# TensorE walks the turns over the edges in loops, and six turns move from the mixing stage to the key stage

## The chip, the cores and the metric

The kernel runs on one core of a Trainium2 chip. Its metric is the time of one execution on the device in microseconds; three runs of the kernel before gave 1978.74, 1978.78 and 1986.1 us, so its median is 1978.78 us. The engines are called by the profile's names: PE (TensorE, with its weight loads as PEld), DVE (VectorE), ACT (ScalarE), POOL (GpSimd) and SP (the engine that only issues transfers here). Each has its own queue of instructions, and they wait for each other by counting semaphores.

## The reference, cut to what matters

N = 6250 nodes have 256 values each; E = 100000 edges carry a source and a destination, sorted by destination. The destinations are drawn as 6250 u^2, so the low nodes have many edges and the high ones few.

```python
xn = layernorm(x)                                    # (6250, 256)
neigh_sum = segment_sum(xn[src], dst)                # sum of the sources' rows for each destination
neigh_mean = neigh_sum / maximum(degree, 1)
g = relu(concat([xn, neigh_mean]) @ W + b); g = g / norm(g)

q, k, v = split(rmsnorm(xn) * g_pre @ w_qkv)         # 4 heads of 32
q = softmax(q, over the 32 of a head) * scale
k = softmax(k, over all nodes and 4 memory columns)
context = k^T v                                      # one 32 x 32 per head
mix = rmsnorm((q @ context) @ w_out + b_out) * g_out + xn

x = x + g + mix
x = x + top_2_of_8_experts(layernorm(x))             # 256 -> 1024 -> 256, gelu
```

The softmax of k runs over all nodes. So the context needs the keys of all 49 tiles of 128 nodes, and the outputs can begin only after it.

## The kernel before, in words

**The gather.** The kernel first normalises x and multiplies it by the lower half of W; the result z lies in HBM. POOL then gathers the rows of z in order of the edges: 784 indirect transfers of 128 rows (L695), four of which make a quad. 196 quads go one after the other into a ring of 8 slots in SBUF. POOL waits before a quad until the turn that last used its slot is counted in p_ready, and it counts the quads that have landed in quads_in.

**A turn.** A turn adds one quad's rows to one tile of 128 destinations. DVE compares the edges' destinations with 0 to 127 and so builds a 0/1 matrix (L1292, four turns ahead), PE multiplies it with the quad's rows (L1813, four fp32 matmuls, which the trace shows as eight), and DVE adds the result to the tile's row in SBUF (L1307). A quad that spans two tiles is used in two turns, so there are 196 + 48 = 244 turns, numbered 0 to 243. Where a turn's quad lies in the ring, and how many quads must have landed, is only known on the chip; PE reads both from a table into registers, eight turns at a time (the loads are recorded at L1800). The PE sequence of a turn is the function turn (it begins with the test j % REGS at L1799), with waits for quads_in, s_built (the matrix) and acc_done (the add of four turns ago).

**What the turns are woven into.** PE, DVE, ACT and SP have their order written out by hand, and the turns stand between the work of two stages.
- The key stage goes over the 49 tiles. Per tile ACT normalises x (L766), PE transposes it (turn_a, L1823), ACT copies it out (L886), SP stores it for later (L501), PE multiplies it to keys and values (kv, L1830), ACT copies these (L890) and DVE keeps the running maximum (L1341). The tiles 1 to 48 carry turns 0 to 89: two each, but every eighth tile only one (turns_of_a, A_EVERY = 8).
- The context has 7 groups of tiles, with the turns 90 to 95 between them.
- The mixing stage goes over the 49 tiles again. Per tile SP loads the normalised tile (L520), PE makes queries and the node's own product (qu, L1879), DVE and ACT make the softmax, PE turns the queries (L1884) and multiplies the ones of the tile before by the context (mix_out, L1889), and DVE and ACT finish the output. Each tile carries three turns: 96 to 242. Tiles 11 to 26 also fold a bias (bfold, L1894). Turn 243 stands at the end.

In the key stage and the context each turn is followed by a small matmul on a spare bank (follow, L1794). After the turns come routing and 56 expert tiles, for which all engines already have a loop over pairs of tiles (the function repeat; its turn back is recorded at L100).

In the kernel before PE's part of the key and mixing stages is written out tile by tile. The other engines' parts of it are, too, and they stay so.

## Time and profile before

| | us |
|---|---|
| median of the runs | 1978.78 |
| span of the profiled execution | 2187.37 |
| of it before the first turn | 89 |
| key stage with turns 0 to 89 | 507 |
| context with turns 90 to 95 | 58 |
| mixing stage with turns 96 to 243 | 636 |
| routing | 206 |
| expert tiles | 691 |

The profiled execution has no other time than its span; it is 208.6 us longer than the median of the runs. The stretches are cut by hand at round times of the trace. Busy time in the profile doesn't count instructions that only wait, branch, compute in registers or issue a transfer; these appear under an engine's queue (PEq, PEldq, SPq). The idle time before an instruction is put down to the one that released it; "issue" is idle time in which nothing is seen to be waited for, and "remote" one whose releaser the profile doesn't find.

### The profile page before, as it was taken

What the parts mean: (1) busy time and instruction counts of PE and PEld (TensorE: products, weight loads), DVE (VectorE), ACT (ScalarE), POOL (GpSimd) and SP (SyncE); (2) the same over time, 40 slices, a digit from 0 to 9 for tenths busy, and PEclk for the clock granted to TensorE, in tenths of its full rate; (3) what the DMA queues carried; (4) which work ended last, traced back from release to release, by engine and by line L of the source; (5) the groups of instructions that cost most, each with busy time, mean ns of one, the idle gap of its engine ahead of it and who ended that gap; (6) DMA issues with size and microseconds to landing.
All of it is one profiled execution on the core that took longest, in us unless ns stands there. A gap on an engine that the chain in (4) does not pass through costs nothing.

```text
span 2187.4 us, 33907 instructions
## 1 busy us (share of the span) xinstructions
PE 1583.7 (72%) x9422; PEld 1361.2 (62%) x9423; DVE 1101.1 (50%) x3043; ACT 900.9 (41%) x1840; POOL 1140.4 (52%) x1141
## 2 busy tenths in 40 slices
PE   6735536546566667867767763548999999999998
PEld 5524435435454544545545543447999999999997
DVE  6512212212234536655555457765666666666664
ACT  6501101101112323323334336554666666666664
POOL 3267666666656666666666612555333333333333
PEclk9868868767878979988888785558999999999999
DMA  7334333333324655566656526537878777877775
GB/s 210 119 100 114 104 101 107 101 97 103 106 81 154 224 165 182 182 180 184 198 182 189 181 76 197 188 135 248 228 215 220 213 221 208 226 214 221 213 221 137
DMA packets 188123, 368.85 MB, mean 169 GB/s; under 512 B 33324, under 2 KB 134172, under 8 KB 173656
## 3 DMA queue, kind: packets, MB, share of 16 engines
q0 software_dynamic: 77296, 252.50, 41.3%
q1 hardware_dynamic: 102992, 113.64, 16.3%
q10 hardware_dynamic: 7736, 1.52, 0.4%
q8 instruction: 45, 0.74, 0.1%
q14 instruction: 54, 0.44, 0.1%
HBM read 287.94 MB, written 80.39 MB: 168 GB/s over the span
## 4 chain that ended last, share of the span: by engine, by line
PE 50%; another core or an unknown queue 17%; DVE 12%; issue 11%; DMA 5%; ACT 3%; SPq 2%; POOL 0%; DVEq 0%; ACTq 0%; POOLq 0%
PE bank L1813 11%; PE bank L2002 5%; PE bank L2003 5%; PE bank L2004 5%; PE bank L2025 5%; PE bank L2024 5%; PE bank L2026 5%; PE bank L1879 3%; DMA xTs<-xnT_d 3%; PE bank L1830 2%; PE bank L1973 1%; DVE acc_lent L1478 1%; DMA z_d<-w2s_lent 1%; DVE acc_lent L1307 1%
## 5 line engine op out<-in xcount | busy, mean ns | idle before, releaser
L695 POOL DMA_INDIRECT w2s_lent<-z_d,edge_tabs_lent x784 | 777.5, 992 | 438.7 <-issue 256.7
L1307 DVE TENSOR_TENSOR acc_lent<-acc_lent,bank 128x258 f32 x244 | 102.7, 421 | 600.6 <-remote 348.8
L1813 PE MATMUL bank<-w2s_lent,S_lent 128*128 x976 | 261.0, 416 | 19.0 <-issue 9.5
L1031 ACT ACTIVATE G<-bank,acc_lent 128x256 f32<-128x256 f32 x448 | 188.3, 472 | 205.9 <-DVE w2s L1670 124.5
L1813 PE MATMUL bank<-w2s_lent,G 128*128 x976 | 265.9, 422 | 3.4 <-issue 3.4
L2024 PE MATMUL bank<-w2s 128*128 128x256 f32 x896 | 264.4, 295 | 0.0
L2002 PE MATMUL bank<-w2s,acc 128*128 128x256 f32 x896 | 260.4, 291 | 2.8 <-issue 2.8
L739 POOL DMA_INDIRECT out_dram<-G,acc_lent x112 | 179.6, 1604 | 158.3 <-DVE G L1650 117.3
L1629 DVE TENSOR_TENSOR acc<-w1s,acc 128x512 fp32r<-128x512 f32 x224 | 155.1, 693 | 200.7 <-ACT acc L1000 174.1
L2004 PE MATMUL bank<-w2s,acc 128*128 128x256 f32 x896 | 254.0, 284 | 0.0
L2025 PE MATMUL bank<-w2s 128*128 128x256 f32 x896 | 253.7, 283 | 0.4 <-issue 0.4
L2026 PE MATMUL bank<-w2s 128*128 128x256 f32 x896 | 253.2, 283 | 0.9 <-issue 0.9
L2003 PE MATMUL bank<-w2s,acc 128*128 128x256 f32 x896 | 253.5, 283 | 0.0
L1813 PEld LDWEIGHTS bank<-w2s_lent,S_lent 128*128 128x128 f32 x976 | 202.5, 211 | 72.6 <-issue 38.5
L1813 PEld LDWEIGHTS bank<-w2s_lent,G 128*128 128x128 f32 x976 | 207.3, 215 | 55.3 <-issue 18.9
L890 ACT ACTIVATE w1s<-bank,r 128x256 f32<-128x256 f32 x49 | 23.3, 475 | 463.8 <-remote 335.0
L723 POOL DMA_DIRECT2D w2s<-w_d x112 | 64.7, 579 | 272.3 <-PE bank L2026 259.5
L1823 PE MATMUL bank<-ident,w2s_lent 128*128 128x128 f32 x98 | 23.7, 330 | 230.0 <-ACT w2s_lent L766 120.2
L2002 PEld LDWEIGHTS bank<-w2s,acc 128*128 128x128 f32 x896 | 171.4, 191 | 3.0 <-issue 2.8
L2026 PEld LDWEIGHTS bank<-w2s 128*128 128x128 f32 x896 | 172.0, 192 | 1.8 <-issue 1.8
L2003 PEld LDWEIGHTS bank<-w2s,acc 128*128 128x128 f32 x896 | 172.9, 193 | 0.0
L2025 PEld LDWEIGHTS bank<-w2s 128*128 128x128 f32 x896 | 171.6, 191 | 1.5
(322 smaller groups left out, 2993.3 us busy)
## 6 DMA issues: line engine op xcount, KB each, us to landing
w2s<-w_d POOLq DMA_DIRECT2D x112, 1024.0 KB
w_d<-w2s_lent SPq DMA_DIRECT2D x64, 256.0 KB
acc_lent<-bucket_d SPq DMA_DIRECT2D x56, 266.0 KB
w2s_lent<-z_d,edge_tabs_lent POOLq DMA_INDIRECT x784
bu_d<-w2s_lent SPq DMA_DIRECT2D x98, 128.0 KB
w2s_lent<-bu_d SPq DMA_DIRECT2D x14, 768.0 KB
w1s<-in_L_ffn_W_dram SPq DMA_DIRECT2D x8, 1024.0 KB
w2s_lent<-in_L_ffn_W_dram SPq DMA_DIRECT2D x32, 256.0 KB
```

Source lines behind the costliest of these rows:

```text
L695: pool.indirect_dma_start(out=ring_rows[:, row % (RING * QUAD), 0:D], out_offset=None, in_=z_d[:, :], in_offset=bass.IndirectOffsetOnAxis( ...
L739: pool.indirect_dma_start(out=out[:, :], out_offset=bass.IndirectOffsetOnAxis(ap=nid[par][:, j:j + 1], axis=0), in_=ys[par][:, j, :], in_o ...
L1031: g = act.activation(raw[q % 2][:, k * MT:(k + 1) * MT], bank[q][:, k * MT:(k + 1) * MT], ACT.Gelu, bias=b1c[1 - par][:, 2 * q + k:2 * q + ...
L1307: dve.tensor_tensor(to, to, bank[j % DEPTH][:, 0:ACCW], ALU.add).then_inc(s["acc_done"], 1)
L1629: dve.tensor_tensor(w1lo[:, :, cols].bitcast(F32R), w1_part(e, q), w1hi[:, :, cols], ALU.subtract).then_inc(s["w1_ready"], 1)
L1813: m = pe.matmul(bank[j % DEPTH][:, 0:ACCW], S_of[j % DEPTH][:, k, :], rows[:, ds(bases[j], ACCW)], start=(k == 0), stop=(k == QUAD - 1))
L2002: pe.matmul(to, hi, x_hi, start=(k == 0), stop=False)
L2003: pe.matmul(to, hi, x_lo, start=False, stop=False)
L2004: m = pe.matmul(to, lo, x_hi, start=False, stop=(k == DC - 1))
L2024: pe.matmul(to[j], hi, w_hi, start=False, stop=False, skip_group_check=True)
L2025: pe.matmul(to[j], hi, w_lo, start=False, stop=False, skip_group_check=True)
L2026: m = pe.matmul(to[j], lo, w_hi, start=False, stop=(c == HC - 1), skip_group_check=True)
```

## The change

TensorE's order for the key stage becomes a function over four tiles that is written out once and then looped 11 times; that of the mixing stage is written out for tiles 1 to 10, looped over 4 times four tiles with the fold and 5 times four tiles without it (the first of each written out), and written out again for the last three. In a loop the numbers that the waits compare with depend on the loop's register, so they are computed in registers. The loads of a turn's place and count move to the head of each group of four or five tiles.

For the loop each tile of the key stage has to have the same number of turns: two. The stage thus takes turns 0 to 95, the context 96 to 101, and the mixing stage begins with turn 102; its first six tiles (SHORT = 6) have two turns and the others three. The numbers follow on all engines, so DVE's order changes as well. The eight matmuls that turn the folded bias stand ahead of tile 27 on PE, and not behind it.

```diff
@@ -408,10 +408,14 @@
 
         def turns_of_a(t):
 
-            return range(2 * t - t // A_EVERY, 2 * (t + 1) - (t + 1) // A_EVERY)
+            return range(2 * t, 2 * t + 2)
+
+        def first_turn_of_b(t):
+
+            return B_FIRST + 3 * t - SHORT if not isinstance(t, int) or t >= SHORT else B_FIRST + 2 * t
 
         def turns_of_b(t):
-            return range(B_FIRST + 3 * t, B_FIRST + 3 * t + 3)
+            return range(first_turn_of_b(t), first_turn_of_b(t + 1))
 
         def in_range(i, ahead):
 
@@ -1437,7 +1441,8 @@
                 b_q2(t)
                 if t:
                     b_o1(t - 1)
-                turn(mine[2])
+                for j in mine[2:]:
+                    turn(j)
                 if SPLIT_AT < t <= SPLIT_END:
                     split_w2(t - SPLIT_AT - 1)
                 if t:
@@ -1792,28 +1797,26 @@
             def follow(spare=7):
 
                 pe.matmul(bank[spare][:, 0:P], before[:, :], ones_b[:, :], start=True, stop=True)
-            bases, needs = {}, {}
-
-            def turn(j):
-
-                if j % REGS == 0:
-                    _, loaded = nc.values_load_multi_w_load_instructions(
-                        rows_i[0:1, base_at + j:base_at + j + REGS], engines=[mybir.EngineType.PE], min_val=0, max_val=(RING - 1) * QW_RING,
-                        skip_runtime_bounds_check_because="a slot of the ring, times the width of one")
-                    bases.update({j + k: v for k, v in enumerate(loaded)})
-                    _, loaded = nc.values_load_multi_w_load_instructions(
-                        rows_i[0:1, need_at + j:need_at + j + REGS], engines=[mybir.EngineType.PE], min_val=1, max_val=QUADS,
-                        skip_runtime_bounds_check_because="a quad's number plus one")
-                    needs.update({j + k: v for k, v in enumerate(loaded)})
-                pe.wait_ge(s["quads_in"], needs[j] & COUNT)
+            regs = {}
+
+            def turn_registers(first, n):
+
+                for what, at, low, high in (("base", base_at, 0, (RING - 1) * QW_RING), ("need", need_at, 1, QUADS)):
+                    _, regs[what] = nc.values_load_multi_w_load_instructions(
+                        rows_i[0:1, ds(at + first, n)], engines=[mybir.EngineType.PE], min_val=low, max_val=high,
+                        skip_runtime_bounds_check_because="a slot of the ring times the width of one, or a quad's number plus one")
+
+            def turn(j, k, bank_of, spare=True):
+
+                pe.wait_ge(s["quads_in"], regs["need"][k] & COUNT)
                 pe.wait_ge(s["s_built"], j + 1)
                 until(pe, s["acc_done"], j + 1 - DEPTH)
-                for k in range(QUAD):
-                    rows = ring[:, k * ACCW:(RING - 1) * QW_RING + (k + 1) * ACCW]
-                    m = pe.matmul(bank[j % DEPTH][:, 0:ACCW], S_of[j % DEPTH][:, k, :], rows[:, ds(bases[j], ACCW)],
-                                  start=(k == 0), stop=(k == QUAD - 1))
+                for q in range(QUAD):
+                    rows = ring[:, q * ACCW:(RING - 1) * QW_RING + (q + 1) * ACCW]
+                    m = pe.matmul(bank[bank_of][:, 0:ACCW], S_of[bank_of][:, q, :], rows[:, ds(regs["base"][k], ACCW)],
+                                  start=(q == 0), stop=(q == QUAD - 1))
                 m.then_inc(s["p_ready"], 1)
-                if j < B_FIRST:
+                if spare:
                     follow()
 
@@ -1832,13 +1835,17 @@
             pe.wait_ge(s["consts_dve"], 3)
             pe.wait_ge(s["kv_weights"], 1)
             turn_a(0)
-            for i in range(NT - 1):
-                mine = turns_of_a(i)
-                turn(mine[0])
-                turn_a(i + 1)
-                for j in mine[1:]:
-                    turn(j)
-                kv(i)
+
+            def four_tiles_a(m):
+
+                turn_registers(8 * m, 8)
+                for k in range(4):
+                    i = 4 * m + k
+                    turn(2 * i, 2 * k, 2 * k % DEPTH)
+                    turn_a(i + 1)
+                    turn(2 * i + 1, 2 * k + 1, (2 * k + 1) % DEPTH)
+                    kv(i)
+            repeat(pe, None, four_tiles_a, 0, (NT - 1) // 4)
             kv(NT - 1)
             pe.wait_ge(s["kv_dve"], NT)
@@ -1858,8 +1865,9 @@
                                   kv_all[0:rows, ds(8 * g + j, 1), HID:KVW].rearrange("p o w -> p (o w)"),
                                   start=False, stop=last, skip_group_check=True)
                 m.then_inc(s["ctx_mm"], 1)
+            turn_registers(CTX_FIRST, 6)
             for g in range(6):
-                turn(CTX_FIRST + g)
+                turn(CTX_FIRST + g, g, (CTX_FIRST + g) % DEPTH)
                 ctx_mm(g)
...
-            for t in range(NT):
-                mine = turns_of_b(t)
-                f = t - FOLD_AT
-                if f == 0:
-                    pe.wait_ge(s["w1_in"], 16 * EXPERTS)
+
+            def tile_b(t, k, j, n=3, bank_of=0, fold=None):
+
                 qu(t)
-                turn(mine[0])
-                if t:
-                    mix_out(t - 1)
-                turn(mine[1])
-                if 0 <= f < 2 * EXPERTS:
-                    bfold(f // 2, f % 2)
-                turn(mine[2])
+                turn(j, k, bank_of, spare=False)
+                mix_out(t - 1) if not isinstance(t, int) or t else None
+                turn(j + 1, k + 1, (bank_of + 1) % DEPTH, spare=False)
+                if fold:
+                    bfold(*fold)
+                if n == 3:
+                    turn(j + 2, k + 2, (bank_of + 2) % DEPTH, spare=False)
                 turn_q(t)
-                if f == 2 * EXPERTS:
-                    pe.wait_ge(s["bf_evac"], 2 * EXPERTS)
-                    for c in range(HC):
-                        m = pe.matmul(bank[5][:, c * EXPERTS:(c + 1) * EXPERTS], bacc[0:EXPERTS, c * P:(c + 1) * P], ident[0:EXPERTS, 0:EXPERTS],
-                                      start=True, stop=True)
-                    m.then_inc(s["b1_mm"], 1)
+
+            def plain_tiles_b(first, end):
+
+                j0, j1 = first_turn_of_b(first), first_turn_of_b(end)
+                turn_registers(j0, j1 - j0)
+                for t in range(first, end):
+                    mine = turns_of_b(t)
+                    tile_b(t, mine[0] - j0, mine[0], len(mine), mine[0] % DEPTH)
+
+            def four_tiles_b(first, m, fold=False):
+
+                j = first_turn_of_b(first) + 12 * m
+                turn_registers(j, 12)
+                for k in range(4):
+                    tile_b(4 * m + (first + k), 3 * k, j + 3 * k, 3, (first_turn_of_b(first) + 3 * k) % DEPTH,
+                           (2 * m + k // 2, k % 2) if fold else None)
+            for first in range(0, FOLD_AT, 5):
+                plain_tiles_b(first, first + 5)
+            pe.wait_ge(s["w1_in"], 16 * EXPERTS)
+            repeat(pe, None, lambda m: four_tiles_b(FOLD_AT, m, True), 0, EXPERTS // 2)
+            pe.wait_ge(s["bf_evac"], 2 * EXPERTS)
+            for c in range(HC):
+                m = pe.matmul(bank[5][:, c * EXPERTS:(c + 1) * EXPERTS], bacc[0:EXPERTS, c * P:(c + 1) * P], ident[0:EXPERTS, 0:EXPERTS],
+                              start=True, stop=True)
+            m.then_inc(s["b1_mm"], 1)
+            repeat(pe, None, lambda m: four_tiles_b(AFTER_FOLD, m), 0, (NT - AFTER_FOLD) // 4)
+            plain_tiles_b(AFTER_FOLD + (NT - AFTER_FOLD) // 4 * 4, NT)
             mix_out(NT - 1)
-            turn(TURNS - 1)
+            turn_registers(TURNS - 1, 1)
+            turn(TURNS - 1, 0, (TURNS - 1) % DEPTH, spare=False)
             pe.wait_ge(s["acc_done"], TURNS)
 
...
-CTX_FIRST = B_FIRST - 6
-A_EVERY = (NT - 1) // (2 * (NT - 1) - CTX_FIRST)
+CTX_FIRST = 2 * (NT - 1)
+B_FIRST = CTX_FIRST + 6
+SHORT = B_FIRST + 3 * NT - (TURNS - 1)
 
 # ---- launch: one core; inputs and outputs as the reference has them ----
```

Three places show what moves. The first is VectorE in the key stage, at the eighth tile. acc_lent is the sum of all tiles, bank3 the result of a turn from PE, the comparison to G builds the matrix of a later turn, and L1341 (L1345 after) is the tile's maximum. Before:

```order
L1341 TENSOR_TENSOR w2s_lent<-w1s,w2s_lent 128x128 [waits kv_dve,kv_act]
L1307 ISA [waits acc_done,p_ready]
L1307 TENSOR_TENSOR acc_lent<-acc_lent,bank2 128x258
L1292 TENSOR_TENSOR G<-iota,edge_tabs_lent 128x512
L1341 TENSOR_TENSOR w2s_lent<-w1s,w2s_lent 128x128 [waits kv_dve,kv_act]
```

After:

```order
L1345 TENSOR_TENSOR w2s_lent<-w1s,w2s_lent 128x128 [waits kv_dve,kv_act]
L1311 ISA [waits acc_done,p_ready]
L1311 TENSOR_TENSOR acc_lent<-acc_lent,bank2 128x258
L1296 TENSOR_TENSOR G<-iota,edge_tabs_lent 128x512
L1311 ISA [waits acc_done,p_ready]
L1311 TENSOR_TENSOR acc_lent<-acc_lent,bank3 128x258
L1296 TENSOR_TENSOR G<-iota,edge_tabs_lent 128x512
L1345 TENSOR_TENSOR w2s_lent<-w1s,w2s_lent 128x128 [waits kv_dve,kv_act]
```

The eighth tile has a second add and comparison ahead of its maximum.

The second place is TensorE at the end of the first mixing tile; bank6 takes the turned queries and bank4 the queries of the next tile. Before, from the last matmul of the second turn (bank1) over the third (bank2):

```order
L1813 MATMUL bank1<-w2s_lent,S_lent 128x258
L1808 REGISTER_ALU
L1813 ISA [waits acc_done,s_built,quads_in]
L1813 MATMUL bank2<-w2s_lent,G 128x258
L1813 ISA
L1813 MATMUL bank2<-w2s_lent,G 128x258
L1813 ISA
L1813 MATMUL bank2<-w2s_lent,G 128x258
L1813 ISA
L1813 MATMUL bank2<-w2s_lent,G 128x258
L1884 MATMUL bank6<-ident,w2s_lent 128x128 [waits q_ready]
L1879 MATMUL bank4<-w2s_lent,xTs 128x384 [waits qu_evac,xb_in]
```

After, from the last matmul of the first turn (bank2) over the second (bank3):

```order
L1816 MATMUL bank2<-w2s_lent,G 128x258
L1811 REGISTER_ALU
L1816 ISA [waits acc_done,s_built,quads_in]
L1816 MATMUL bank3<-w2s_lent,G 128x258
L1816 ISA
L1816 MATMUL bank3<-w2s_lent,G 128x258
L1816 ISA
L1816 MATMUL bank3<-w2s_lent,G 128x258
L1816 ISA
L1816 MATMUL bank3<-w2s_lent,G 128x258
L1892 MATMUL bank6<-ident,w2s_lent 128x128 [waits q_ready]
L1887 MATMUL bank4<-w2s_lent,xTs 128x384 [waits qu_evac,xb_in]
```

There is no third turn, and the transpose of the queries follows the second.

The third place is TensorE at the head of a group of mixing tiles, tile 11. Before:

```order
L1879 MATMUL bank4<-w2s_lent,xTs 128x384 [waits qu_evac,xb_in,w1_in]
L1879 MATMUL bank4<-w2s_lent,xTs 128x384
L1808 REGISTER_ALU
L1813 ISA [waits acc_done,s_built,quads_in]
L1813 MATMUL bank2<-w2s_lent,G 128x258
L1813 ISA
```

After, in the loop:

```order
L1805 TENSOR_LOAD w2s_lent
L1805 ISA
L1805 TENSOR_LOAD w2s_lent
L1884 ISA
L85 REGISTER_ALU [waits xb_in]
L1887 MATMUL bank4<-w2s_lent,xTs 128x384 [waits qu_evac]
L1887 MATMUL bank4<-w2s_lent,xTs 128x384
L1811 REGISTER_ALU
L1812 REGISTER_ALU [waits quads_in]
L85 REGISTER_ALU [waits s_built]
L1816 ISA [waits acc_done]
L1816 MATMUL bank2<-w2s_lent,G 128x258
```

The loads stand ahead of the tile, and the one instruction that waited for three semaphores has become three.

## Rows read from the trace of the kernel before

**Rows 1.** The page: busy time, share, instructions; a DMA queue: packets, MB, share.

```profile
PE 1583.7 (72%) x9422; PEld 1361.2 (62%) x9423; DVE 1101.1 (50%) x3043; ACT 900.9 (41%) x1840; POOL 1140.4 (52%) x1141
...
q8 instruction: 45, 0.74, 0.1%
```

**Rows 2.** Busy time in stretches: from:to, length, then each engine (instructions).

```profile
core 0: us, PE busy (x) PEld busy (x) DVE busy (x) ACT busy (x) POOL busy (x), PEclk, DMA share, GB/s
...
89.00:596.00 507.00, 260.16 (x1100) 207.84 (x1100) 107.93 (x241) 59.18 (x143) 341.29 (x347) 0.76 0.37 104
596.00:654.00 58.00, 33.18 (x172) 25.99 (x172) 18.00 (x34) 9.47 (x12) 35.16 (x34) 0.76 0.29 83
654.00:1290.00 636.00, 453.29 (x1570) 314.96 (x1569) 345.38 (x936) 215.38 (x390) 401.09 (x405) 0.85 0.58 179
...
1496.00:2187.00 691.00, 676.50 (x5607) 671.47 (x5605) 437.05 (x905) 440.12 (x884) 253.85 (x231) 0.99 0.78 215
```

**Rows 3.** Groups by line: busy us, mean ns | idle us before, by releaser.

```profile
L695 POOL DMA_INDIRECT w2s_lent<-z_d,edge_tabs_lent x784 | 777.5, 992 | 438.7 <-issue 256.7 <-remote 88.0 <-PE bank L1813 77.6
```

**Rows 4.** Timeline, 113 to 158 us: start, us, instruction [idle before <-releaser].

```profile
113.66 1.08 PE L1830 MATMUL bank<-G,xTs 128*128 128x256 f32 x4
...
120.59 0.22 PE L1794 MATMUL bank<-ones_b,before 128*128 128x128 bf16 x1
...
149.68 0.95 POOL L695 DMA_INDIRECT w2s_lent<-z_d,edge_tabs_lent  x1 [0.30 <-issue]
...
153.76 0.47 ACT L890 ACTIVATE w1s<-bank,r 128x256 f32<-128x256 f32 x1 [47.84 <-remote]
...
157.47 1.16 POOL L695 DMA_INDIRECT w2s_lent<-z_d,edge_tabs_lent  x1 [6.85 <-remote]
```

**Rows 5.** Waits: who for whom, us in total, times, longest us.

```profile
DVE acc_lent L1307 <- remote: 348.8, 45, 27.0
ACT w1s L890 <- remote: 335.0, 20, 47.8
...
POOL w2s_lent L695 <- issue: 256.7, 667, 33.6
```

**Rows 6.** Timeline around 414 us, PE's key matmuls.

```profile
411.74 1.08 PE L1830 MATMUL bank<-G,xTs 128*128 128x256 f32 x4
...
416.48 1.08 PE L1830 MATMUL bank<-G,xTs 128*128 128x256 f32 x4
```

**Rows 7.** Query matmuls of mixing tiles 1, 2 and 7; idle time before all.

```profile
652.64 2.67 PE L1879 MATMUL bank<-w2s_lent,xTs 128*128 128x384 f32 x4 [0.46 <-DVE w2s_lent L1384]
...
661.92 1.46 PE L1879 MATMUL bank<-w2s_lent,xTs 128*128 128x384 f32 x4
...
735.38 2.13 PE L1879 MATMUL bank<-w2s_lent,xTs 128*128 128x384 f32 x3
...
  DMA xTs<-xnT_d: 78.1, 32
```

**Rows 8.** By source line, PE's queue: duration ns min/median/max, first and last start.

```profile
L100 PEldq FUSED_REGOPS  x24: 68/68/68, 1574.2 to 2132.8; - x24
...
L100 PEldq ALU_OP  x24: 32/32/32, 1598.4 to 2156.7; - x24
L100 PEldq COMPARE_BRANCH  x24: 76/213/238, 1598.5 to 2156.8; - x24
...
L85 PEldq EVENT_SEMAPHORE  x585: 51/51/4847, 14.8 to 2165.5; - x195
...
L1800 PEldq TENSOR_LOAD <-w2s_lent x31: 587/592/1007, 90.8 to 1288.2; - x31
```

**Rows 9.** Timeline of the expert loop where PE turns back.

```profile
1719.83 0.28 PE L2003 MATMUL bank<-w2s,acc 128*128 128x256 f32 x1
1719.95 0.28 PE L2004 MATMUL bank<-w2s,acc 128*128 128x256 f32 x1
```

**Rows 10.** DMA issues: KB each, median us from issue to landing.

```profile
small<-in_L_mix_g_pre_dram ACTq DMA_DIRECT2D x2, 0.5 KB, 2.1
```

More of the change, by code:

```diff
@@ L2079 @@
 AFTER_FOLD = FOLD_AT + 2 * EXPERTS
-B_FIRST = TURNS - 1 - 3 * NT
-CTX_FIRST = B_FIRST - 6
-A_EVERY = (NT - 1) // (2 * (NT - 1) - CTX_FIRST)
+CTX_FIRST = 2 * (NT - 1)
+B_FIRST = CTX_FIRST + 6
+SHORT = B_FIRST + 3 * NT - (TURNS - 1)
 _INS = ["x", "src", "dst", "L0_gnn_W", "L0_gnn_b", "L0_mix_w_qkv", "L0_mix_mem_kv", "L0_mix_w_out", "L0_mix_b_out",
```

## The prediction, made before the result was known

> **What bounds the kernel now.** I read the page's busy shares first: over the span of 2187.4 us no engine is full, TensorE has 72% and POOL 52% [rows 1]. So the kernel has stages with different limits, and the table of stretches comes next [rows 2]. The reader is to see there five parts that the prediction can leave alone or not. The first 89 us (normalisation) and everything after 1290 us (206 us of routing, 691 us of expert tiles with 676.5 us of TensorE busy) hold no turn. All turns lie in the three stretches between: the key stage, 507 us; the context, 58 us; the mixing stage, 636 us.
>
> In these 1201 us the list by line gives POOL's gathers, 784 of them at 992 ns, with 438.7 us idle before them [rows 3]. The timeline shows that 0.30 us of idle time stands before each gather even when nothing holds it [rows 4]. So a gather costs 0.99 + 0.30 = 1.29 us, a quad (four gathers) 5.17 us, and all 784 cost 1013 us. 235 us of the 438.7 are this pace; the wait list has one of 33.6 us, the idle time before the first gather; the other 170 us are waits for a free ring slot [rows 5]. POOL is thus at its own pace for 1013 of some 1183 us from the first gather to the last, and what TensorE does in this time counts only as far as it lets the ring fill.
>
> What fills it is seen in the timeline around 117 to 157 us [rows 4]. TensorE's rows end at 120.8 us, but ScalarE sees the end of the key matmul of 113.66 us only at 153.76 us, after 47.84 us of idle time that the profile can't put down to a queue. TensorE's next transposes wait for ScalarE behind that, the turns wait behind the transposes, eight quads fill the ring, and POOL stands still for 6.85 us. The ring swallowed 41 of these 48 us. Such late ends are the largest entries of the wait list: 348.8 us on the adds of VectorE and 335.0 us on ScalarE's copies of keys [rows 5]. The trace doesn't show their cause, and I assume that the change doesn't touch it.
>
> When it isn't held, TensorE is much quicker than POOL: two key tiles in a row start their key matmuls 4.74 us apart (411.74 and 416.48 us) [rows 6], where the key stage has 507 / 48 = 10.56 us a tile. In the mixing stage the distance is small: 636 / 49 = 12.98 us a tile, against 9.3 us between the first two tiles [rows 7], which is the shortest the first ones show. There the load of the next tile stands in the chain: the query matmuls sat idle 78.1 us for it, 32 times [rows 7].
>
> **The moved turns.** Key tiles 8, 16, ... 48 get a second turn: six turns more, 96 instead of 90. Mixing tiles 1 to 6 lose one each, and from the seventh on every tile starts with the same turn as before. Each turn takes eight matmul records, one add and one comparison that builds the matrix for four turns later; all of these are only moved, and so are the quads that they need. At POOL's pace the total doesn't change, so the term is 0. Its two ends are these. Upper: a turn costs the key stage its own pace of 507 / 90 = 5.63 us, 33.8 us for six, and the mixing stage gives nothing back, since its tiles have another limit: +33.8 us. Lower: the key stage is paced by its tiles (10.56 us whether with one turn or two) and the six turns are free, while the mixing stage gives back 12.98 / 3 = 4.33 us each: -26.0 us. I take 0, since POOL's 1013 us are by far the largest row of this stretch. The first six mixing tiles took 735.4 - 652.6 = 82.8 us, 13.8 us each [rows 7]; with two turns their gathers need at most 2 x 5.17 = 10.3 us a tile, and 9.3 us has been reached with three turns, so TensorE can keep up; a shortfall of some us goes into the ring, which holds 8 x 5.17 = 41 us.
>
> On VectorE the removed turn takes 0.42 + 0.69 us out of the tile, ahead of the work on the output of the tile before, and on the key side the same two instructions stand before the maximum of the tile; both are under the gathers. SP and POOL issue what they did, in the same order.
>
> **The loops.** Nothing of TensorE's arithmetic is added. By the listing of the order, four key tiles had 42 register instructions and loads of registers in a row and now have 68 in a pass; four mixing tiles had 64 and now have 98 (with the fold) or 88. With 11, 3 and 4 passes after the ones that are written out, that is 286 + 102 + 96 = 484 more. In this kernel such instructions take 32 ns (ALU) to 51 ns (wait) each [rows 8], together 15.5 to 24.7 us, and 18 turns back at 32 + 213 + 68 ns add 5.6 us. Against it the pairs of loads fall from 31 to 26, at 592 ns a load: -5.9 us. So this edit lies between -5.9 us (all else hidden) and +30.3 us (all of it on the path). I take +2 us. What hides it: TensorE's queue runs ahead of the matmuls wherever no wait holds it, and where one holds it, the instructions before the wait are done in that time. The expert loop, which is written in the same way, shows it: its matmuls follow each other without idle time at the turn back (1719.83 to 1720.31 us) [rows 9]. Only the two or three instructions behind the last wait of a turn are late, and behind them stands POOL's pace. If that cover is gone, every turn pays about 0.1 us.
>
> The Trainium skill has a rule that speaks against this edit ("Runtime: NRT & Kernel Launch", Instruction fetch mechanics): "A taken branch whose target isn't in the current 2-page window forces a DMA fetch of the target page before execution can continue". By it every pass could begin with a stall. The rows of the existing loop say otherwise for a body of this size: its 24 branches took 76 to 238 ns [rows 8]. With that the sum stays as it is.
>
> One wait moves: the eight small matmuls that turn the folded bias now stand before the queries of tile 27, not behind its turns, and so wait for VectorE's last fold (a few us, once). What is queued behind is that tile; the ring hides it. 0 us.
>
> **Sum.** 2187.4 + 0 + 2 = 2189.4 us on the profiled execution. The runs have a median of 1978.8 us, 208.6 us less than the profile's span, and the profile doesn't tell from which stage they are missing. 1978.8 minus the stretches without turns (986 us) leaves 993 us for what took 1201 us; even without one ring wait the gathers' 1013 us would fill that, which is one more reason for POOL's pace. If the missing time is in the gathers themselves, the mixing stage is nearer to its tile limit, and the moved turns can cost. I carry the +2 us over unscaled: 1981 us.
>
> **The rivals.**
> First, slower: the mixing tiles are bound by their own chain, not by POOL. Place: the first six tiles and the 28 looped ones. The key stage pays 33.8 us for its six turns, the first mixing tiles give back no more than (13.8 - 9.3) x 6 = 27 us, and a looped tile has 34 / 4 = 8.5 instructions more, 0.43 us at 51 ns, 12 us over 28. Together +19 us: 1998 us. It decides once a tile's chain is longer than the 10 to 13 us of its gathers. For it: the 78.1 us before the query matmuls, and the unknown pace of the unprofiled gathers. Against it: 12.98 us a tile against 9.3.
> Second, faster: the key stage is paced by the late ends that come once a tile, not by gathers. Then its second turns are free and the mixing stage gives back 26 us: 1953 us; half of it, 1966 us. For it: 335.0 us of ScalarE's idle time [rows 5]. Against it: POOL is at its pace for 448 of the stage's 507 us (347 gathers at 1.29) [rows 2].
> Third, faster: the late ends come from the long stream of instructions, and loops shorten it. A third of the 170 us of ring waits would be 57 us: 1922 us. Only the size of that wait speaks for it; the page has 45 instruction packets, and none of 0.74 MB in all looks like a load [rows 1].
> Fourth, slower: each of the 18 turns back waits for code to be loaded. The nearest small load of the page took 2.1 us [rows 10], so 38 us less what the ring hides: up to 2017 us. The 238 ns speak against it. This is the mechanism of the Trainium skill's rule quoted above.
>
> **How the numbers follow.** The bound between a change and none is 0.5%, 9.9 us, about what a measurement of this kernel tells. Chances: the forecast 0.46, the first rival 0.27, the second 0.19, the third 0.04, the fourth 0.04. The second and third make the 0.23 for faster, the first and fourth the 0.31 for slower, the forecast the 0.46 for the same. The forecast's own range is 1971 to 1991 us. The range for 8 in 10 must reach into both main rivals: down to 1953, the lower end of the moved turns, and up to 2009, the first rival's 1998 and a part of the loops' upper end: 1953 to 2009 us.
>
> **What would show it.** In the new profile the sum of the stretches of key, context and mixing stage should stay within 10 us of 1201 us, with the boundary between key and mixing stage some 25 to 34 us later and the first six mixing tiles at 9 to 11 us each. Ring waits should stay near 170 us, the branches of the new loops under 0.3 us. The step on the moved turns is wrong if the boundary moves and the last gather moves with it, or if it doesn't move at all. The step on the loops is wrong if idle time before the turns' matmuls put down to nothing ("issue") grows by more than 10 us. The whole is wrong if the late ends become rarer or more frequent, for then 170 us are open in either direction.

## The result, and the profile after

The changed kernel takes 2017.41 us (median of 4 runs, 2010.52 to 2020.09), the kernel before 1978.76 us; the ratio is 1.0179, with a 95% interval of 1.0159 to 1.0198. It is 38.65 us slower. The forecast of 1981 us was wrong, and the time lies outside the range of 1953 to 2009 us.

The profiled execution of the changed kernel has a span of 2015.7 us, as long as its runs. That of the kernel before had been 208.6 us longer than its runs. So the two can't be subtracted stage by stage. The kernel before was profiled a second time (experiment e1), and this second profile (span 1982.7 us) is the one to compare with. Busy time of the changed kernel:

```profile
PE 1600.3 (79%) x9428; PEld 1362.4 (68%) x9429; DVE 1101.1 (55%) x3043; ACT 898.7 (45%) x1840; POOL 1139.1 (57%) x1141
```

TensorE has 1600.3 us, VectorE 1101.1 us and POOL 1139.1 us, almost what they had [rows 1]. Most of the loss is idle time. The stretches of the changed kernel in the order key stage, context, mixing stage, then routing and experts (from:to, length, busy time of each engine, clock, DMA share, GB/s):

```profile
89.00:553.00 464.00, 314.00 (x1164) 232.44 (x1164) 120.07 (x266) 62.12 (x149) 347.91 (x358) 0.84 0.41 118
553.00:585.00 32.00, 26.45 (x156) 22.19 (x157) 13.37 (x21) 6.21 (x7) 24.99 (x24) 0.92 0.32 92
585.00:1172.00 587.00, 440.43 (x1562) 309.89 (x1562) 347.01 (x954) 220.73 (x405) 404.01 (x404) 0.87 0.63 194
1172.00:1320.00 148.00, 74.99 (x550) 69.05 (x551) 119.68 (x621) 99.64 (x244) 83.17 (x85) 0.54 0.61 201
1320.00:2015.00 695.00, 679.77 (x5659) 675.25 (x5657) 440.66 (x921) 444.86 (x893) 260.48 (x240) 0.99 0.77 218
```

The same stretches of the kernel before, in its second profile, which answer to [rows 2]:

```profile
89.00:528.00 439.00, 300.11 (x1119) 222.98 (x1120) 114.66 (x255) 62.92 (x149) 327.79 (x339) 0.83 0.42 119
528.00:556.00 28.00, 23.31 (x151) 19.62 (x149) 13.43 (x22) 5.59 (x6) 22.21 (x20) 0.99 0.31 90
556.00:1135.00 579.00, 449.19 (x1607) 313.01 (x1607) 351.03 (x958) 221.49 (x405) 427.39 (x427) 0.90 0.66 203
1135.00:1290.00 155.00, 82.39 (x592) 76.06 (x593) 122.88 (x638) 102.56 (x249) 87.44 (x89) 0.53 0.60 196
1290.00:1982.00 692.00, 676.96 (x5617) 672.48 (x5616) 439.44 (x912) 442.19 (x889) 255.75 (x236) 0.99 0.79 218
```

The key stage with its six more turns is 25 us longer, the context 4 us, and the mixing stage, which has six turns fewer, is 8 us longer and not shorter. After it the changed kernel needs 843 us and the kernel before 847. So 37 us are lost ahead of routing and none behind it (the two spans differ by 33 us, the medians by 38.65).

Who waits for whom in the mixing stage tells what bounds it (us in total, times, longest). The kernel before, second profile:

```profile
POOL w2s_lent L695 <- issue: 117.7, 346, 5.2
PE bank L1813 <- POOLq L683: 56.4, 23, 6.2
PE bank L1879 <- DMA xTs<-xnT_d: 53.5, 21, 6.9
```

The changed kernel:

```profile
POOL w2s_lent L699 <- issue: 112.6, 332, 5.0
PE bank L1887 <- issue: 64.8, 11, 7.0
PE bank L1887 <- DMA xTs<-xnT_d: 42.6, 16, 4.9
...
POOL w2s_lent L699 <- PE bank L1816: 17.9, 13, 4.5
```

Before, TensorE waits 56.4 us for quads (POOLq L683 counts the landed ones): POOL is the slower one, and TensorE has this much to spare with its turns in the old places. After, that wait is gone, and instead 64.8 us stand before 11 query matmuls (L1887), put down to "issue", that is, to nothing seen. Now POOL waits for TensorE (17.9 us in this stage). Over the whole kernel its gathers have this idle time:

```profile
L699 POOL DMA_INDIRECT w2s_lent<-z_d,edge_tabs_lent x784 | 776.9, 991 | 303.8 <-issue 243.8 <-DMA w2s_lent<-z_d,edge_tabs_lent 36.6 <-PE bank L1816 23.4
```

The end of the stage says the same. The last gather of the kernel before starts at 1124.54 us, and the last turn (TensorE, L1813) waits for its quad:

```profile
1124.54 0.95 POOL L695 DMA_INDIRECT w2s_lent<-z_d,edge_tabs_lent  x1 [0.30 <-issue]
...
1129.40 3.63 PE L1813 MATMUL bank<-w2s_lent,G 128*128 x8 [2.35 <-POOLq L683]
```

In the changed kernel the last turn comes 27 us after the last gather, and ten turns are still to be worked off:

```profile
1136.32 0.95 POOL L699 DMA_INDIRECT w2s_lent<-z_d,edge_tabs_lent  x1 [0.30 <-issue]
...
1163.59 3.18 PE L1816 MATMUL bank<-w2s_lent,G 128*128 x8
```

What holds TensorE is found under its queue. The register loads at the head of each group (L1805: durations in ns min/median/max, first and last start), in six stretches of the changed kernel:

```profile
L1805 PEldq TENSOR_LOAD <-w2s_lent x24: 587/591/625, 91.3 to 506.8; - x24
...
L1805 PEldq TENSOR_LOAD <-w2s_lent x2: 830/833/836, 551.8 to 552.7; - x2
...
L1805 PEldq TENSOR_LOAD <-w2s_lent x2: 2415/2420/2426, 586.1 to 588.6; - x2
...
L1805 PEldq TENSOR_LOAD <-w2s_lent x2: 1342/1444/1547, 639.2 to 640.8; - x2
...
L1805 PEldq TENSOR_LOAD <-w2s_lent x18: 2864/3063/4273, 696.9 to 1085.0; - x18
...
L1805 PEldq TENSOR_LOAD <-w2s_lent x2: 2169/2170/2172, 1129.9 to 1132.1; - x2
```

The loads of eight in the key stage take 0.59 us, as before [rows 8]. The six at the context take 0.83, the 10 from entry 102 2.4, the 14 from 112 1.4, the 12 of each group of four tiles 3.1, the 9 from 234 2.2 us. The number doesn't explain it (14 are quicker than 9), the start does: 8m, 96 and 112 are multiples of four, 102, 234 and the loops' 126, 138, ... aren't. At the head of a group this is seen on TensorE at 745 us:

```profile
744.98 0.32 PE L1892 MATMUL bank<-ident,w2s_lent 128*128 128x128 f32 x1
751.99 2.92 PE L1887 MATMUL bank<-w2s_lent,xTs 128*128 128x384 f32 x4 [6.69 <-issue]
...
763.33 1.46 PE L1887 MATMUL bank<-w2s_lent,xTs 128*128 128x384 f32 x4
```

The turned queries (L1892) are done at 745.3 us, and the next tile's queries begin 6.7 us later, behind a pair of loads of 2.9 and 3.5 us. The gap costs a little more than itself. The four query matmuls behind it take 2.92 us, those of the tile after it, without a gap, 1.46 us. TensorE's granted clock stood at its full level (1.00, 2.4 GHz) before the gap and at the lower one (0.50, 1.2 GHz) behind it:

```profile
740.00:745.00 5.00, 5.00 (x20) 2.62 (x18) 3.89 (x13) 0.31 (x1) 3.77 (x5) 1.00 0.89 267
752.00:755.00 3.00, 3.00 (x5) 1.79 (x6) 0.00 (x0) 0.00 (x0) 2.08 (x4) 0.50 0.93 271
```

### The profile page after: what moved, and what is told of

Same layout as the page of the kernel before. It is cut to its first block, busy times and chain, and to the rows that moved or that the text cites. A ratio compares the mean times of both kernels' runs of the same rounds, so it can differ in the third digit from the quotient of the medians.

```text
span 2015.7 us, 34258 instructions
## 1 busy us (share of the span) xinstructions
PE 1600.3 (79%) x9428; PEld 1362.4 (68%) x9429; DVE 1101.1 (55%) x3043; ACT 898.7 (45%) x1840; POOL 1139.1 (57%) x1141
## 4 chain that ended last, share of the span: by engine, by line
PE 44%; DVE 7%; DMA 7%; issue 5%; SPq 2%; ACT 2%; POOL 1%; DVEq 0%; POOLq 0%; ACTq 0%
PE bank L1816 5%; PE bank L2030 5%; PE bank L2031 5%; PE bank L2032 5%; PE bank L2053 5%; PE bank L2052 5%; PE bank L2054 5%; DMA xTs<-xnT_d 5%; PE bank L1887 3%; PE bank L2001 1%; POOL bucket_d L713 1%; SPq L545 1%; PE bank L1902 1%; PE bank L2041 1%; DVE w2s_lent L1420 1%
## 5 line engine op out<-in xcount | busy, mean ns | idle before, releaser
L1816 PE MATMUL bank<-w2s_lent,G 128*128 x976 | 284.3, 443 | 79.8 <-POOLq L687 76.6
L1816 PE MATMUL bank<-w2s_lent,S_lent 128*128 x976 | 267.0, 422 | 65.2 <-POOLq L687 59.0
L1816 PEld LDWEIGHTS bank<-w2s_lent,G 128*128 128x128 f32 x976 | 213.9, 224 | 147.2 <-issue 109.5
L1816 PEld LDWEIGHTS bank<-w2s_lent,S_lent 128*128 128x128 f32 x976 | 201.5, 211 | 125.1 <-issue 90.6
L1887 PE MATMUL bank<-w2s_lent,xTs 128*128 128x384 f32 x196 | 101.8, 655 | 107.4 <-issue 64.8
L2030 PEld LDWEIGHTS bank<-w2s,acc 128*128 128x128 f32 x896 | 170.3, 190 | 5.4 <-issue 5.4
L2053 PEld LDWEIGHTS bank<-w2s 128*128 128x128 f32 x896 | 171.6, 191 | 1.5
L2052 PEld LDWEIGHTS bank<-w2s 128*128 128x128 f32 x896 | 172.1, 192 | 0.0
L2054 PEld LDWEIGHTS bank<-w2s 128*128 128x128 f32 x896 | 172.0, 192 | 0.0
```

The lines of the kernel that those rows point to most:

```text
L1816: m = pe.matmul(bank[bank_of][:, 0:ACCW], S_of[bank_of][:, q, :], rows[:, ds(regs["base"][k], ACCW)], start=(q == 0), stop=(q == QUAD - 1))
L1887: m = pe.matmul(bank[4][:, 0:HID + D], xTs[:, c * P:(c + 1) * P], w_qu[:, c, :], start=(c == 0), stop=(c == DC - 1))
L2030: pe.matmul(to, hi, x_hi, start=(k == 0), stop=False)
L2052: pe.matmul(to[j], hi, w_hi, start=False, stop=False, skip_group_check=True)
L2053: pe.matmul(to[j], hi, w_lo, start=False, stop=False, skip_group_check=True)
L2054: m = pe.matmul(to[j], lo, w_hi, start=False, stop=(c == HC - 1), skip_group_check=True)
```

## The experiments

Two theories stood against each other after the result. A: the register loads of the mixing stage are slow because of where they start, and take TensorE's spare time. B: the six moved turns cost in the key stage and aren't given back. A third, C, was the loops' register instructions and turns back. All ratios are to runs of the kernel before on the same chip, taken together with those of the experiment; the interval is of 95%. The diffs are cut to the lines that matter, and `...` stands for what is left out.

**e1, the kernel before once more.** No edit.

> The kernel before, unchanged, for a second profile. The first profile was 208.6 us longer than its runs, the changed kernel's only as long as its runs. If the late matmul ends (348.8 us before VectorE's adds put down to nothing) belong to that one profiled execution, this profile has a span near 1977 us, a gather stretch of about 1010 us (784 x 1.29) and no such waits. If they belong to the long stream of written-out instructions, they come again and the span is again near 2187 us. Time: 1979 us in both.

Measured: 0.9993 (0.9979 to 1.0008), span 1982.7 us, gathers from 90.6 to 1125.5 us:

```profile
L695 POOL DMA_INDIRECT w2s_lent<-z_d,edge_tabs_lent x784 | 777.4, 992 | 291.1 <-issue 244.8 <-DMA w2s_lent<-z_d,edge_tabs_lent 41.1 <-PE bank L1813 5.2
```

POOL has 291.1 us idle against 438.7 [rows 3]; of it 33.6 us stand ahead of the first gather, and the waits put down to TensorE are 5.2 us, none longer than the 0.3 us that stand before every gather. The late ends of [rows 4, 5] don't come again, though the instruction stream is the same. They belonged to that one execution.

**e2, mixing loads from multiples of four.** In the changed kernel:

```diff
             def turn_registers(first, n, skip=0):
+                n = (n + skip + 3) // 4 * 4
...
-                        rows_i[0:1, ds(at + first, n)], ...
+                        rows_i[0:1, ds(at + first - skip, n)], ...
+                    regs[what] = regs[what][skip:]
...
-                turn_registers(j, 12)
+                turn_registers(j, 12, first_turn_of_b(first) % 4)
```

> The changed kernel, but each register load of the mixing stage begins at a multiple of four entries of the table and takes whole fours (16 entries where it took 12). Theory of the slow loads: the pairs of loads at the 13 heads, 6.0 us each in the changed kernel's profile (2.9 + 3.1), fall to about 1.1 us an instruction, 2.2 us a pair, so some 45 us of PE's time at the tile heads go, and the kernel comes back to 1978 to 1990 us. Theory of the moved turns (the key stage pays for six more turns at POOL's pace and the mixing stage gives nothing back): unchanged, 2010 to 2018 us. Theory of waits for registers and turns back: unchanged too.

Measured: 1985.37 us, ratio 1.0018 (1.0001 to 1.0035). The loads of 12 from 100 and of 16 from 124, 136, ...:

```profile
L1806 PEldq TENSOR_LOAD <-w2s_lent x2: 846/847/848, 586.8 to 587.7; - x2
...
L1806 PEldq TENSOR_LOAD <-w2s_lent x18: 1102/1107/2141, 693.9 to 1055.8; - x18
```

More entries, and a third of the time. At the same head as above the queries now wait for their data alone:

```profile
737.39 0.27 PE L1894 MATMUL bank<-ident,w2s_lent 128*128 128x128 f32 x1
740.03 2.58 PE L1889 MATMUL bank<-w2s_lent,xTs 128*128 128x384 f32 x4 [2.36 <-DMA xTs<-xnT_d]
```

1.6 of the 1.8% come back. A holds; B and C can have no more than what is left.

**e3, the moved turns alone.** In the changed kernel the loops are written out and the loads are those of the kernel before:

```diff
+                if j % REGS == 0:
+                    load_eight(j)
+                k = j % REGS
...
-            repeat(pe, None, four_tiles_a, 0, (NT - 1) // 4)
+            written_out(four_tiles_a, (NT - 1) // 4)
```

> The moved turns alone: PE's order is that of the changed kernel, but written out without a loop, with registers loaded eight turns at a time at multiples of eight as in the kernel before. Theory of the slow loads: 1975 to 1985 us, as before. Theory of the moved turns: most of the 38.7 us, 2005 to 2018 us. Theory of the loops' register instructions and branches: 1979 us.

Measured: 1979.74 us, 0.9990 (0.9977 to 1.0004): nothing. Its key stage, context and mixing stage:

```profile
89.00:553.00 464.00, 314.55 (x1171) 234.06 (x1172) 120.01 (x266) 62.83 (x149) 346.95 (x361) 0.84 0.42 119
553.00:583.00 30.00, 24.87 (x153) 20.82 (x152) 13.80 (x22) 5.59 (x6) 23.60 (x22) 0.96 0.33 96
583.00:1130.00 547.00, 431.41 (x1559) 300.95 (x1557) 344.88 (x946) 221.10 (x405) 400.11 (x403) 0.91 0.68 208
```

The key stage pays 25 us and the mixing stage gives back 32. B falls as a cause by itself. This kernel has the order and the turns of the changed one, so its mixing stage is the one to set against the changed kernel's 587 us. TensorE's waits for quads and for the tiles' data in it:

```profile
PE bank L1896 <- DMA xTs<-xnT_d: 58.4, 24, 5.5
...
PE bank L1823 <- POOLq L687: 22.0, 11, 5.8
```

Moving six turns out of the stage also takes waits for quads out of it: 22.0 us are left of 56.4. The changed kernel has none of them and 42.6 us of the others. Its matmuls in this stage are as many, but take 440.43 us against 431.41, at a granted clock of 0.87 against 0.91.

**e4, loops and slow loads with the turns where they were.** The key stage is as before; the mixing stage (turns 96 to 243) has the loops and the loads of 12 from 126, 138, ...:

```diff
-            return range(2 * t, 2 * t + 2)
+            return range(2 * t - t // A_EVERY, 2 * (t + 1) - (t + 1) // A_EVERY)
...
-CTX_FIRST = 2 * (NT - 1)
-B_FIRST = CTX_FIRST + 6
+B_FIRST = TURNS - 1 - 3 * NT
+CTX_FIRST = B_FIRST - 6
```

> The loops of the mixing stage alone, with the loads of 12 registers, and the turns where they were (0 to 89, 90 to 95, 96 to 243); the key stage stays written out with loads of eight. Theory of the slow loads: nearly all of the loss, 2005 to 2018 us, with loads of 2.2 to 4.3 us at entries 126, 138, ... as in the changed kernel. Theory of the moved turns: 1979 to 1985 us.

Measured: 2003.32 us, 1.0112 (1.0094 to 1.0130), slower by 21.8 us. This is less than A said. Its stretches:

```profile
89.00:535.00 446.00, 308.40 (x1144) 229.96 (x1144) 116.63 (x258) 63.52 (x150) 334.50 (x343) 0.82 0.42 118
535.00:562.00 27.00, 19.16 (x124) 16.01 (x124) 11.36 (x19) 4.81 (x6) 21.19 (x20) 0.95 0.32 93
562.00:1157.00 595.00, 447.75 (x1607) 316.23 (x1607) 350.57 (x957) 220.84 (x405) 418.90 (x422) 0.87 0.64 196
```

Between e4 and the changed kernel stand the moved turns: 18 us more in the key stage, 5 in the context, and only 8 given back by the mixing stage. In e3, where that stage goes at POOL's pace, six turns fewer gave back 32 us. With slow loads it goes at its tiles' own pace, and a turn less is worth little. So the moved turns cost nothing alone and some 13 us beside the slow loads (1.0179 less 1.0112, of 1980 us). The waits for quads say why. With the old turns the slow loads could use up 45 of 56.4 us, and this is left in e4:

```profile
PE bank L1820 <- POOLq L687: 11.6, 6, 6.6
```

With the moved turns there were 22.0 us to use, and all are gone.

This pair of loads, in e4, has the same 15 entries twice, from entry 96 and from entry 111:

```profile
L1805 PEldq TENSOR_LOAD <-w2s_lent x2: 1577/1582/1587, 559.0 to 560.6; - x2
...
L1805 PEldq TENSOR_LOAD <-w2s_lent x2: 3651/3714/3777, 611.2 to 614.9; - x2
```

**e5, slow loads in the key stage too.**

```diff
-                turn_registers(8 * m, 8)
+                turn_registers(8 * m - 2, 10)
+                for what in regs:
+                    regs[what] = regs[what][2:]
```

> The changed kernel, with slow loads in the key stage as well: each of its 12 groups loads 10 entries from 8m - 2 where it loaded 8 from 8m. By the mixing stage's loads (0.24 us an entry when the start is no multiple of four) each takes 2.4 us where it took 0.59, so PE's key stage has 12 x 2 x 1.8 = 43 us more. Theory: the cover decides. The key stage goes at POOL's pace (gaps of 0.3 us before the gathers, ring waits of about 2 us per 100 us), PE has several us to spare in each tile, and the time stays within 5 us of the changed kernel's (2012 to 2023 us). Rival, that such a load costs its length wherever it stands: 2055 to 2062 us.

Measured: 2015.45 us, 1.0171 (1.0147 to 1.0194), the same as the changed kernel. The 24 loads took 2.4 us each:

```profile
L1805 PEldq TENSOR_LOAD <-w2s_lent x24: 2397/2406/2817, 90.5 to 508.8; - x24
```

That is 24 x 1.8 = 44 us more on TensorE, and none of it is seen in the time: the gathers cover it. The same load costs nothing in one stage and bounds the other.

**e6, the changed kernel written out, with its own loads.** All three loops of TensorE's turns go, as here:

```diff
-            repeat(pe, None, four_tiles_a, 0, (NT - 1) // 4)
+            written_out(four_tiles_a, (NT - 1) // 4)
```

> The changed kernel without a loop on PE: the same order and the same loads (10, 14, 12 and 9 entries from the same starts), written out. If the starts and counts of the loads make them slow, they take 2.9 us again and the time is 2008 to 2018 us, at most some 6 us under the changed kernel. If it is that the loop computes the address of the load in a register, or that the load stands behind a turn back, the loads take 0.85 us or less and the time is 1978 to 1986 us.

Measured: 2014.14 us, 1.0174 (1.0153 to 1.0195). The loop isn't the cause, neither of the time nor of the length of the loads:

```profile
L1805 PEldq TENSOR_LOAD <-w2s_lent x18: 2866/3086/4517, 698.7 to 1086.4; - x18
```

**e7, the loads behind the queries.** The pair moves from ahead of qu to behind it.

```diff
                 qu(t)
+                if group:
+                    turn_registers(j, group)
```

> The changed kernel with each group's pair of loads behind the matmuls of the group's first queries (qu) and not ahead of them; the loads themselves the same, 2.9 us each. If the loads cost by what stands behind them, the start of a tile's chain (queries, softmax, turned queries), most of the loss comes back: the matmuls of the queries (2.7 us) run under the loads, and only the tile's first turn is late, 1988 to 2000 us. If the loads cost by PE's time alone, 2010 to 2018 us.

Measured: 2034.44 us, 1.0271 (1.0254 to 1.0287). Both expectations were wrong: it is 17 us slower than the changed kernel. At the head of a group:

```profile
843.77 2.10 PE L1887 MATMUL bank<-w2s_lent,xTs 128*128 128x384 f32 x4 [2.34 <-DMA xTs<-xnT_d]
851.68 0.80 PE L1816 MATMUL bank<-w2s_lent,G 128*128 x1 [5.82 <-issue]
```

Ahead of the queries the loads run while TensorE would wait for the tile's data anyway. Behind them TensorE first waits for the data (2.34 us) and then for the loads (5.82 us), and three turns and the output of the tile before stand behind that. The place hides a part; I had named the wrong one.

**e8, a pair of loads for each tile.** The same 6 us for four tiles, in four pieces:

```diff
             def tile_b(t, k, j, n=3, bank_of=0, fold=None):
+                turn_registers(j, n)
+                k = 0
...
-                turn_registers(j0, j1 - j0)
...
-                turn_registers(j, 12)
```

> The changed kernel with a pair of loads of 2 or 3 entries at the head of every mixing tile in place of one pair of 9 to 14 at the head of a group: about 0.75 us an instruction, 1.5 us a tile, the same sum over four tiles (6 us). If the sum of the loads' time decides, 2010 to 2018 us. If a late start of 6 us costs more than four of 1.5 us, since a short one hides behind the wait for the tile's data, 1985 to 2002 us.

Measured: 1992.29 us, 1.0054 (1.0036 to 1.0073). Loads of 3 entries took 0.77 us. Spread, the same sum costs a third: 1.5 us fit under the wait for the tile's data (2.4 us in e2's row), 6 us don't.

**e9, e2 written out.** The edit of e6 on the kernel of e2, here the loop without the fold:

```diff
-            repeat(pe, None, lambda m: four_tiles_b(AFTER_FOLD, m), 0, ...)
+            written_out(lambda m: four_tiles_b(AFTER_FOLD, m), ...)
```

> The kernel of e2 (mixing loads from multiples of four, whole fours) without a loop on PE. e2 was 0.18% over the kernel before, the moved turns alone 0.1% under it. If the rest of e2 is the loops' register instructions and turns back: 1978 to 1981 us. If it is its loads (1.1 us an instruction against 0.59, at 13 heads): 1983 to 1988 us, as e2.

Measured: 1984.13 us, 1.0023 (1.0010 to 1.0035), as e2. It has no loop either, so the small rest of e2 isn't its loops; its loads are what it has beyond e3 (0.9977 to 1.0004).

**e10, aligned loads for each tile.** The edit of e8 on the kernel of e2; bank_of is the turn's number modulo four:

```diff
             def tile_b(t, k, j, n=3, bank_of=0, fold=None):
+                turn_registers(j, n, bank_of)
+                k = 0
```

> The changed kernel with its loops; each mixing tile loads its own 2 or 3 turns, from a multiple of four and in whole fours (4 or 8 entries, 0.3 or 0.59 us an instruction). A load at a head is short enough to hide behind the wait for the tile's data: 1979 to 1985 us. If the number of load instructions costs, since each stands before the wait for the tile's data, 1986 to 1995 us, near e8's 1992.

Measured: 1983.63 us, 1.0016 (1.0000 to 1.0033). It hides, but no better than e2.

**e11, a loop in the key stage alone.** The mixing stage is written out, with loads of eight from multiples of eight:

```diff
             def turn(j, k, bank_of, spare=True):
+                if not spare:
+                    if j % REGS == 0:
+                        turn_registers(j, REGS)
+                    k = j % REGS
```

> The changed kernel with a loop in the key stage alone, and the mixing stage written out with loads of eight at multiples of eight. The key stage is covered by the gathers (e5: slow loads there cost nothing), so 1976 to 1982 us, the same as the kernel before and as the moved turns alone. If the key loop costs something by itself, 1983 us or more.

Measured: 1981.99 us, 1.0005 (0.9992 to 1.0019), no difference.

**e12, the kernel before with slow loads and nothing else.**

```diff
+                    early = 2 if j >= B_FIRST else 0
...
-                        rows_i[0:1, base_at + j:base_at + j + REGS], ...
+                        rows_i[0:1, base_at + j - early:base_at + j + REGS], ...
```

> The kernel before, and of the change nothing but slow loads: from turn 96 on each of the 19 pairs of loads reads 10 entries from two entries earlier than it did, and so from a start that is no multiple of four. Theory of the slow loads: 2.4 us an instruction, 19 x 2 x 1.8 = 68 us more on PE, and a kernel slower by some 20 to 35 us (2000 to 2015 us), since e4 lost 21.8 us with 86 us of loads. If the loss needs the changed order or the loops, 1979 to 1985 us.

Measured: 2006.26 us, 1.0130 (1.0108 to 1.0152), slower by 25.4 us, with no loop and no turn moved. The loads of the places, which had taken 0.59 us, in 17 of the 19 pairs:

```profile
L1801 PEldq TENSOR_LOAD <-w2s_lent x17: 2397/2677/4443, 616.4 to 1134.8; - x17
```

Summed over all 62 of them the loads of the turns take 123.9 us on TensorE, where those of e1 take 40.6: 83 us more of loads cost 25 us, and the waits took up the rest.

None of these kernels is faster than the kernel before; e3 and e11 are as fast.

## Why the prediction was wrong

**The step that failed** is a term of the sum on the loops: "the pairs of loads fall from 31 to 26, at 592 ns a load: -5.9 us". There are 26 pairs, but the 22 loads of 9, 10 and 12 entries at starts that are no multiple of four take 2.2 to 4.3 us each. By the medians above: 24 x 0.59 + 2 x 0.83 + 2 x 2.42 + 2 x 1.44 + 18 x 3.06 + 2 x 2.17 + 2 x 0.30 = 84 us, against 62 x 0.59 = 37 us. The term was +47 us and not -5.9 (each load summed by itself: 85.3 against 40.6 us in e1, +45). I took the duration from a row in which every load had eight entries from a multiple of eight [rows 8], and didn't see that the change alters both. It was the one operation whose shape the change altered, and its cost should have been bounded from both sides. e2, e6 and e12 show the term.

The Trainium skill has a figure for it that I passed over, in the very section that I quoted ("Runtime: NRT & Kernel Launch", Instruction fetch mechanics): a load of registers costs about 200 ns a register, even in bulk. An estimate by this figure is 2.4 us for 12 registers; here they took 2.9 us where the start is no multiple of four. At a multiple of four the measurement differs from the figure: 16 took 1.1 us, where the estimate would be 3.2 us.

**The cover** was the second part of that step: "TensorE's queue runs ahead of the matmuls wherever no wait holds it". At the twelve heads of the mixing stage it was 0.3 us ahead at most: at six the first load begins after TensorE's last matmul has ended, at the others no more than 0.3 us before. A pair is 6 us. What does hide a part are waits that stood there anyway, and they were too few. Against e3, in the mixing stage, 64.8 us of idle time before the queries are new; the waits for the tiles' data fall by 15.8 us (58.4 to 42.6) and those for quads by 22.0 us (to none), and the matmuls take 9.0 us more at the lower clock. That makes +36 us, where the stretches differ by 40 (547 and 587 us).

**POOL's pace** as the bound of the kernel before was right, and clearer than the first profile showed: in the second its gathers run from 90.6 to 1125.5 us, where 784 x 1.29 us are 1013. But the 170 us of ring waits were those of one execution. The forecast that they stay was wrong: the second profile has 5.2 us of waits for TensorE, the changed kernel 23.4. The warning was in the prediction (993 us left for these stretches), and I didn't draw from it that TensorE was close behind POOL in the mixing stage. The sum of the three stretches, which was to stay at 1201 us, is 1083 us, against 1046 us in e1.

**The moved turns** at 0 were right (e3), and the boundary of the stages moved by 25 us as said (528 to 553 us). The first six mixing tiles went to the 9 to 11 us that were forecast: from 591.03 to 652.89 us, 10.3 us a tile. The prediction named the condition of this 0 ("the mixing stage is nearer to its tile limit, and the moved turns can cost"), and the slow loads brought it about: +13 us beside them (e4). Its test would have misled: the boundary moved by 25 us and the last gather by 12 (1124.54 to 1136.32 us), which was to speak against this step. In e3 the boundary moves as far and the last gather comes at 1119.7 us, so it is the loads that delay it.

**The loops' register instructions** at a few us were right: e6 against the changed kernel, e9 against e2 and e11 against the kernel before each show no difference that these runs can tell. The turns back take what the expert loop's took [rows 8]:

```profile
L100 PEldq COMPARE_BRANCH  x42: 76/208/236, 174.5 to 1985.0; - x42
```

So the fourth rival, a stall for code at each turn back, falls: the longest is 236 ns. The rule of the Trainium skill on taken branches (the same section) is about targets outside a window. A pass of these loops and the experts' has some 260 to 450 of TensorE's instructions in the trace, and none longer was run, so the runs neither bear the rule out nor speak against it.

**The rivals.** The first came nearest in mechanism: mixing tiles bound by their own chain after a key stage that pays for its turns. But that holds only with the slow loads (in e3 the stage goes at POOL's pace), and its 1998 us had the wrong price: 12 us for register instructions where the loads put 47 us on TensorE. The upper end of the fourth, 2017 us, is the measured time by chance alone. The second fell with e3. The third found nothing: e6 has the long stream and the changed kernel's time.

**The test that I named** looked at the wrong place. I wanted to see "issue" time before the turns' matmuls; it stood before the query matmuls, 64.8 us on L1887, since the loads moved ahead of them. In e12, where the loads stand ahead of turns, it is where the test looked for it: 57.8 us before the turns' matmuls in the mixing stage.

**Open:** why a load's time follows its start, and why single loads took longer still. Open too is what the late ends in the first profile were. They came in one of the fourteen profiled executions (two of the kernel before, the changed kernel's and those of e2 to e12).

## What to carry to other kernels

When a loop regroups instructions that look unchanged, compare the operands of every one of them, the registers' loads too: a different count or start is a different instruction, and a duration read from the old shape is a guess. For loads like these, take fours from multiples of four; where that can't be, split a long load, or put it where the engine waits for data anyway. When a profile's span is far above the median of the runs, take a second one before reading a bound from its waits.

## What the runs showed of the hardware

The time of a load into TensorE's registers follows its start. From a start that is no multiple of four entries each entry costs 0.24 us: 9 took 2.17, 10 took 2.40, 12 took 2.87 (the shortest in the loops) and 15 took 3.65 us. From a multiple of four, 8 took 0.59, 12 took 0.85 and 16 took 1.10 us, some 0.26 for each four. Of 14 entries from 112 and 15 from 96, the odd ones at the end seem to cost 0.24 each again (1.34 and 1.58 us). Entries are 4 bytes, and the tables begin at multiples of 256 entries. Starts two and three past a multiple of four were seen, one past it only in short loads (e8). In the mixing stage single loads of 12 took up to 4.3 us against the shortest 2.87, which the start doesn't explain; in the key stage, where the DMA engines are 0.41 busy and not 0.63, the same kind of load stayed within 2.40 and 2.82 us (e5). That the transfers cause it isn't shown.

TensorE's granted clock was lower behind the gap at 745 us: 1.00 before it, 0.50 behind it, with the four query matmuls at 2.92 us in place of 1.46.
